# The last gather of every fourth block brought by SyncE's single-row copies instead of a GpSimd gather

## Chip, cores and metric

One core of one Trainium2 chip. The metric is the device time of one execution in microseconds (us). The kernel before takes 615.87 us, the median of 3 runs (612.99 to 616.21).

## What is computed

A recommendation model's top: for each of 2048 samples, 32 rows of 256 floats are taken from 32 embedding tables, all pairwise dot products of the 32 rows are formed, and three dense layers follow. Cut to what matters:

```python
e = jnp.stack([tbl_f[ids[:, f]] for f in range(32)], axis=1)     # [2048, 32, 256]
dots = jnp.einsum('bnd,bmd->bnm', e, e)
z = dots[:, iu, ju]                                               # pairs i < j: 496 numbers
h = jnp.concatenate([z, dense_ctx], axis=1)                       # with 16 dense inputs: 512
h = jnp.maximum(h @ W_top1 + b_top1, 0.0)
h = jnp.maximum(h @ W_top2 + b_top2, 0.0)
y = h @ W_top3
```

All in float32. The tables have 1000, 1250 or 12500 rows; 2048 random ids choose the rows.

## The kernel before, in words

The samples go through in 32 blocks of 64 (`BLOCK`). A block needs 64 x 32 rows of 1 KB. The fields go in units of four (`FPU`); a unit of a block is 256 rows and is fetched by two gathers (`SUBS`), each of 128 rows, one row to a partition. Blocks 0 to 3 have 8 units (`ALL`), so 16 gathers; from block 4 on there are 7 units (`UNITS`), 14 gathers, because the last four fields (`PICKS`, tables of 1000 rows) are fetched in another way: their tables lie on the chip, split into a high and a low part, and TensorE picks the rows by multiplying with one-hot matrices (`pick`). `unit(t, u)` numbers all units: there are 228, so 456 gathers.

POOL (GpSimd) issues the gathers, line 192, in order. Unit x goes into `rows[x % 8]`; from the ninth unit on POOL waits until PE has transposed unit x - 8 (line 190). The gather's row numbers are in `index`, which DVE makes once at the start by adding `base` to `raw` (`make_index`, line 403).

PE (TensorE) follows an order written out by hand (lines 292 to 316): for each unit it waits for its gathers and makes four transposes (line 205) into one of three PSUM buffers (`TURNS`), and between units it does a part of other work: the dot products of the block before (`gram`, line 252), the picks for blocks four ahead (lines 234, 236), and once in two blocks layers 1 to 3 (lines 268, 279, 286). Layer 1 of turn n comes in block 2n + 3 at unit 1; layer 3 of turn n in block 2n + 4 at unit 4. ACT (ScalarE) copies each transposed unit out of PSUM (line 327) and also, in one fixed order with it, spreads the ids that the picks need (`spread_ids`, line 339), takes the picks out of PSUM (line 343, `take_pick`) and puts them in place (line 350). In block 2n + 4, ACT spreads ids after unit 3 and takes a pick after unit 4; PE's pick at unit 6 waits for that copy. DVE makes the one-hots (line 410), regroups the dot products (line 422), and takes the scores (line 441).

SP (SyncE) issues all ordinary DMAs on one queue, in order. At the start: `base` and the first index part (lines 129, 131), the rest (line 132), tables 0 and 1 (line 140), ids 0 and 1 (line 136), two dense loads (line 144), table 2, the weights; then, after a wait for `low_done`, table 3. Then comes a loop of 16 turns, one for two blocks:

```python
for n in range(TILES):
    if n + 2 < JOBS // 2:
        sp.wait_ge(ids_spread, 2 * (n + 1))
        load_ids(n + 2)
    if n + 2 < TILES:
        sp.wait_ge(l1_done, n + 1)
        load_dense(n + 2)
    sp.wait_ge(score_ready, n + 1)
    sp.dma_start(out[n:n + 1, :], score[:, n % 2, :]).then_inc(stored[n % 2], 16)
```

`JOBS // 2` is 14, so turns 0 to 11 load ids. The ids loaded in turn n are first spread in block 2n + 4 after unit 3; turn n begins when score n - 1 is stored, which is in block 2n + 2.

Of the kernel before, what the change touches and what calls it, by code (L numbers as in the profile page):

```python
# [8 lines left out]
U32 = mybir.dt.uint32  # L9
ALU = mybir.AluOpType  # L10
ACT = mybir.ActivationFunctionType

P = 128
# [3 lines left out]
FPU = 4  # L17
# [2 lines left out]
GROUP = 256  # L20


def dlrm_tower(nc, index_t, base_t, pick_ids, pick_tables, dense_t, table, w1_t, b1_t, w2, b2_t, w3_t, out):

# [3 lines left out]
    D = table.shape[1]  # L30
# [4 lines left out]
    UNITS = (N_FIELDS - PICKS) // FPU  # L35
    SUBS = BLOCK // SPG
    GATHERS = ALL * SUBS
    BLOCKS = index_t.shape[1] // GATHERS
    FQ, TQ = BLOCK // QUAD, P // QUAD
    TILES = BLOCKS // 2  # L40
    BPG = GROUP // BLOCK
# [4 lines left out]
    VC = 8  # L46
    VP = V // VC
    ROWS, COLS, TURNS = 8, 3, 3
    PIECES = VC * D // 512
    assert HALVES == 2 and ND <= N_FIELDS and VP * VC == V and VP <= P and BPG == PICKS == 4  # L50

    def units(t):
        return ALL if t < BPG else UNITS

    def unit(t, u):
        return ALL * min(t, BPG) + UNITS * max(t - BPG, 0) + u

    def gram_parts(t):
        return {2: (0, 4), 3: (4, 8), 4: (8, 12), 5: (12, 16)} if t % 2 == 1 else {1: (0, 6), 2: (6, 11), 3: (11, 16)}

    with ExitStack() as ctx:
        def sb(name, shape, dt=F32):
            return ctx.enter_context(nc.sbuf_tensor(name, shape, dt))
# [4 lines left out]
        def sem(name):  # L68
            return ctx.enter_context(nc.semaphore(name))

        raw = sb("raw", [P, BLOCKS, GATHERS], U32)
        base = sb("base", [P, GATHERS], U32)
        index = sb("index", [P, BLOCKS, GATHERS], U32)
        rows = [sb(f"rows{r}", [P, SUBS, D]) for r in range(ROWS)]
        cols = [sb(f"cols{r}", [P, HALVES, BLOCK, N_FIELDS]) for r in range(COLS)]
        stage = [sb(f"stage{g}", [P, HALVES, GROUP, PICKS]) for g in range(2)]
        pairs = [sb(f"pairs{p}", [P, KC, P]) for p in range(2)]
# [8 lines left out]
        identity = sb("identity", [P, P])  # L86
# [16 lines left out]

        index_loaded = [sem(f"index_loaded{i}") for i in range(2)]
        index_ready = sem("index_ready")
        gathered = [sem(f"gathered{r}") for r in range(ROWS)]
        transposed, cols_ready = sem("transposed"), sem("cols_ready")
        gram_done, pairs_ready = sem("gram_done"), sem("pairs_ready")
# [18 lines left out]
        @block.sync  # L127
        def _(sp):
            sp.dma_start(base[:, :], base_t).then_inc(index_loaded[0], 16)
            index_v = index_t.rearrange("p (t g) -> p t g", t=BLOCKS)  # L130
            sp.dma_start(raw[:, 0:1, :], index_v[:, 0:1, :]).then_inc(index_loaded[0], 16)
            sp.dma_start(raw[:, 1:BLOCKS, :], index_v[:, 1:BLOCKS, :]).then_inc(index_loaded[1], 16)

            def load_ids(m):
                g, j = m // 2, 2 * (m % 2)
                sp.dma_start(pick_id[m % 2][:, :, :], pick_ids[g, j:j + 2, :].unsqueeze(0).broadcast_to([VP, 2, GROUP])
                             ).then_inc(ids_loaded[m % 2], 16)

            def load_table(j):
                sp.dma_start(table_raw[j], pick_tables[j].rearrange("(p c) d -> p c d", c=VC)  # L140
                             ).then_inc(table_loaded[j], 16)

            def load_dense(n):
                sp.dma_start(pairs[n % 2][0:ND, 0, :], dense_t[n]).then_inc(dense_loaded[n % 2], 16)

            load_table(0)
            load_table(1)
            load_ids(0)
            load_ids(1)
            sp.wait_ge(pairs_zeroed, 2)  # L150
            load_dense(0)
            load_dense(1)
            sp.wait_ge(table_loaded[0], 16)
            load_table(2)
            sp.wait_ge(table_loaded[1], 16)
            sp.dma_start(w1_sb[:, :, :], w1_t).then_inc(w1_loaded, 16)
            sp.dma_start(b1_sb[:, :], b1_t).then_inc(w_loaded, 16)
            sp.dma_start(b2_sb[:, :], b2_t).then_inc(w_loaded, 16)
            sp.dma_start(w3_sb[:, :], w3_t).then_inc(w_loaded, 16)
            sp.dma_start(w2_sb[:, :, :], w2.rearrange("(m p) n -> p m n", p=P)).then_inc(w_loaded, 16)  # L160
            sp.wait_ge(low_done, 3 * PIECES)
            load_table(3)
            for n in range(TILES):
                if n + 2 < JOBS // 2:
                    sp.wait_ge(ids_spread, 2 * (n + 1))
                    load_ids(n + 2)
# [5 lines that stand above are left out]
            for p in range(2):  # L172
                sp.wait_ge(stored[p], 16 * (TILES // 2))

        @block.gpsimd
        def _(pool):
            pool.memset(identity[:, :], 0.0).then_inc(identity_zeroed, 1)
            pool.iota(row_number[:, :], [[1, VC]], base=0, channel_multiplier=VC,
                      allow_small_or_imprecise_dtypes=True).then_inc(numbers_ready, 1)
            pool.wait_ge(identity_zeroed, 1)  # L180
            pool.affine_select(out=identity[:, :], in_=identity[:, :], compare_op=ALU.not_equal, fill=1.0,
                               base=0, pattern=[[-1, P]], channel_multiplier=1).then_inc(identity_ready, 1)
            pool.wait_ge(index_ready, 1)
            for t in range(BLOCKS):
                if t == 1:
                    pool.wait_ge(index_ready, 2)
                for u in range(units(t)):
                    x = unit(t, u)
                    if x >= ROWS:
                        pool.wait_ge(transposed, x - ROWS + 1)  # L190
                    for k in range(SUBS):
                        pool.indirect_dma_start(  # L192
                            out=rows[x % ROWS][:, k, :], out_offset=None, in_=table,
                            in_offset=bass.IndirectOffsetOnAxis(ap=index[:, t, SUBS * u + k:SUBS * u + k + 1], axis=0),
                        ).then_inc(gathered[x % ROWS], 16)

        @block.tensor
        def _(pe):
            def transposes(x):
                pe.wait_ge(gathered[x % ROWS], 16 * SUBS * (x // ROWS + 1))  # L200
                if x >= TURNS:
                    pe.wait_ge(cols_ready, x - TURNS + 1)
                for h in range(HALVES):
                    for k in range(SUBS):
                        last = pe.transpose(ps_turn[x % TURNS][:, h, SPG * k:SPG * (k + 1), :],  # L205
                                            rows[x % ROWS][:, k, h * P:(h + 1) * P], identity[:, :])
                last.then_inc(transposed, 1)

            def split_table(j):
# [5 lines left out]
                hi_v = table_hi[:, j, :, :].rearrange("p c d -> p (c d)")  # L215
                for i in range(PIECES):
                    x = PIECES * j + i
                    if x >= 2:
# [6 lines left out]
            def pick(q, h):  # L225
                j = q % PICKS
                if h == 0:
                    pe.wait_ge(one_hot_ready, q + 1)
                    if q < PICKS:
                        pe.wait_ge(lo_ready, PIECES * (3 if j < 2 else 4))  # L230
                    if q >= 1:
# [40 lines left out]
            def layer2(n):  # L272
                pe.wait_ge(hidden1_ready, n + 1)
                if n == 0:
                    pe.wait_ge(w_loaded, 64)
                    pe.wait_ge(lo_ready, PIECES * PICKS)
                for m in range(M2C):
# [122 lines left out]
        def _(dve):  # L400
            def make_index(t0, t1):
                n = t1 - t0
                dve.tensor_tensor(index[:, t0:t1, :], raw[:, t0:t1, :],
                                  base[:, :].unsqueeze(1).broadcast_to([P, n, GATHERS]), ALU.add).then_inc(index_ready, 1)
# [39 lines left out]
                dve.memset(pairs[p][0:N_FIELDS, 0, :], 0.0).then_inc(pairs_zeroed, 1)  # L444
            dve.wait_ge(index_loaded[0], 32)
            make_index(0, 1)
            dve.wait_ge(index_loaded[1], 16)
            make_index(1, BLOCKS)
            dve.wait_ge(numbers_ready, 1)

            def take_lo(j):
                for i in range(PIECES):
                    x = PIECES * j + i
                    dve.wait_ge(low_done, x + 1)
                    dve.tensor_copy(table_lo[:, j, :, :].rearrange("p c d -> p (c d)")[:, 512 * i:512 * (i + 1)],  # L455
                                    ps_low[x % 2]).then_inc(lo_ready, 1)
# [72 lines left out]
```

## Time and profile before

| | |
|---|---|
| median of 3 runs | 615.87 us |
| the profiled execution | 614.14 us, of which its span 612.3 us |
| PE, PEld busy | 522.7 us (85%), 466.6 us (76%) |
| POOL busy | 432.1 us (71%) |
| DVE, ACT busy | 278.3 us (45%), 209.6 us (34%) |
| DMA engines, mean busy share in the steady part | 3 to 4 tenths |
| granted TensorE clock, mean | 0.964 of full speed |

PE is TensorE's matmuls, PEld its weight loads, DVE VectorE, ACT ScalarE, POOL GpSimd, SPq SyncE's DMA queue. A matmul's end is modelled, so a busy PE is not PE at its peak. "Issue" is time in which an engine waited for nothing that the profile shows. The span is the time from the first to the last instruction of the profiled execution.

### The profile page before, as it was taken

To read this page: it belongs to the slowest core of one execution; us is meant where nothing else is said; L and a number is where in the kernel's file an instruction comes from. 1 tells how busy PE (TensorE), PEld (TensorE's weight loads), DVE (VectorE), ACT (ScalarE), POOL (GpSimd) and SP (SyncE) were. 2 spreads that over 40 slices of the span, in tenths; PEclk is the share of its full clock that TensorE was granted. 3 is DMA by queue.
4 is the path that set the end of the run, shared out by engine and by line. 5 is a ranking of instruction groups with operands and counts; after the bars stand their busy time and mean duration, and the time that the engine had idled before them with its cause. 6 is when DMAs were issued, how large, how long until landed. Compare 5 with 4: busy or idle time off the path is not lost.

```text
span 612.3 us, 24786 instructions
## 1 busy us (share of the span) xinstructions
PE 522.7 (85%) x11392; PEld 466.6 (76%) x11392; DVE 278.3 (45%) x600; ACT 209.6 (34%) x390; POOL 432.1 (71%) x463
## 2 busy tenths in 40 slices
PE   1068998999999999988999898989989897996967
PEld 0054796998889897978889786978878796984857
DVE  0013744827364545555273535556263555426060
ACT  1044233343433334343334224333332333432130
POOL 6767677777777777777777777777777777777600
PEclk9978998999999999998999999999999999998788
DMA  5695443443434343433434343434434333333300
GB/s 155 210 241 191 136 139 107 110 126 107 122 111 125 109 121 112 125 107 108 124 110 123 106 126 111 122 107 112 125 105 122 109 109 108 107 108 111 97 3 1
DMA packets 26411, 72.10 MB, mean 118 GB/s; under 512 B 8426, under 2 KB 9338, under 8 KB 25680
## 3 DMA queue, kind: packets, MB, share of 16 engines
q0 software_dynamic: 21888, 59.80, 35.5%
q1 hardware_dynamic: 4420, 10.72, 5.6%
q8 instruction: 90, 1.47, 1.0%
q14 instruction: 13, 0.11, 0.0%
HBM read 70.48 MB, written 0.01 MB: 115 GB/s over the span
## 4 chain that ended last, share of the span: by engine, by line
PE 65%; DMA 14%; POOL 11%; issue 7%; ACT 1%; DVE 1%; SPq 0%; POOLq 0%; ACTq 0%
PE ps_l L268 18%; PE ps_turn L205 15%; POOL rows L192 11%; PE ps_gram L252 11%; DMA rows<-in_table,index 10%; PE ps_pick L234 7%; PE ps_pick L236 7%; DMA pick_id<-in_pick_ids 5%; PE ps_l L279 2%; PE ps_l L220 1%; PE ps_pick L220 1%; PE ps_l L286 1%; DVE pairs L422 0%; PE ps_l L222 0%; PE ps_pick L222 0%
## 5 line engine op out<-in xcount | busy, mean ns | idle before, releaser
L192 POOL DMA_INDIRECT rows<-in_table,index x456 | 431.2, 946 | 146.3 <-issue 118.8
L422 DVE COPY pairs<-ps_gram 32x112 f32<-32x112 f32 (+1 forms) x504 | 189.1, 375 | 140.9 <-PE ps_gram L252 134.5
L327 ACT COPY cols<-ps_turn 128x512 f32<-128x512 f32 x228 | 132.1, 590 | 314.5 <-PE ps_turn L205 314.1
L205 PE MATMUL ps_turn<-identity,rows 128*128 128x128 f32 x912 | 148.2, 293 | 59.0 <-DMA rows<-in_table,index 44.6
L205 PEld LDWEIGHTS ps_turn<-identity,rows 128*128 128x128 f32 x912 | 104.0, 147 | 74.8 <-DMA rows<-in_table,index 41.2
L252 PE MATMUL ps_gram<-cols 128*32 128x32 f32 x8192 | 113.5, 201 | 22.9 <-issue 21.3
L252 PEld LDWEIGHTS ps_gram<-cols 128*32 128x32 f32 x8192 | 93.4, 111 | 49.9 <-issue 44.4
L410 DVE TENSOR_TENSOR one_hot<-ps_ids,row_number 125x2048 fp32r<-125x2048 f32 x28 | 63.9, 2281 | 139.5 <-ACT ps_ids L339 118.9
L268 PE MATMUL ps_l<-pairs,w_sb 128*128 128x128 f32 x1024 | 121.9, 282 | 3.1 <-DVE score L441 3.1
L268 PEld LDWEIGHTS ps_l<-pairs,w_sb 128*128 128x128 f32 x1024 | 120.5, 199 | 3.6 <-DVE pairs L422 3.6
L234 PE MATMUL ps_pick<-one_hot,table_hi 125*128 125x256 f32 x448 | 115.1, 295 | 0.4 <-ACT stage L343 0.4
L236 PE MATMUL ps_pick<-one_hot,table_lo 125*128 125x256 f32 x448 | 110.2, 284 | 0.0
L234 PEld LDWEIGHTS ps_pick<-one_hot,table_hi 125*128 125x128 f32 x448 | 86.1, 192 | 0.6 <-issue 0.6
L236 PEld LDWEIGHTS ps_pick<-one_hot,table_lo 125*128 125x128 f32 x448 | 86.5, 193 | 0.0
L343 ACT COPY stage<-ps_pick 128x512 f32<-128x512 f32 x28 | 30.6, 1093 | 37.0 <-PE ps_pick L236 37.0
L279 PE MATMUL ps_l<-hidden,w_sb 128*128 128x128 f32 x256 | 31.4, 276 | 1.2 <-ACT hidden L360 1.2
L279 PEld LDWEIGHTS ps_l<-hidden,w_sb 128*128 128x128 f32 x256 | 29.8, 192 | 1.6 <-ACT hidden L360 1.4
L360 ACT ACTIVATE hidden<-ps_l,b_sb 128x128 f32<-128x128 f32 x64 | 18.3, 376 | 10.4 <-PE ps_l L268 10.4
L339 ACT CAST ps_ids<-pick_id 125x256 f32<-125x256 int32 x28 | 10.7, 383 | 28.5 <-DMA pick_id<-in_pick_ids 28.5
L455 DVE CAST table_lo<-ps_l 125x512 fp32r<-125x512 f32 x8 | 5.5, 691 | 29.7 <-PE ps_l L222 29.7
L350 ACT COPY cols<-stage 128x512 f32<-128x512 f32 x28 | 17.4, 622 | 0.2
L433 DVE TENSOR_SCALAR hidden<-ps_l,b_sb 128x128 f32<-128x128 f32 x32 | 9.8, 347 | 13.9 <-PE ps_l L279 13.4
(31 smaller groups left out, 79.1 us busy)
## 6 DMA issues: line engine op xcount, KB each, us to landing
rows<-in_table,index POOLq DMA_INDIRECT x456
pick_id<-in_pick_ids SPq DMA_DIRECT2D x14, 250.0 KB
w_sb<-in_w_t SPq DMA_DIRECT2D x1, 2048.0 KB, 29.9
cols<-in_tbl SPq DMA_DIRECT2D x2, 1000.0 KB
stage<-in_tbl SPq DMA_DIRECT2D x2, 1000.0 KB
w_sb<-in_W_top SPq DMA_DIRECT2D x1, 512.0 KB, 32.6
pairs<-in_dense_t SPq DMA_DIRECT2D x16, 8.0 KB
scores<-score SPq DMA_DIRECT2D x16, 0.5 KB
```

What stands on the lines that cost most here:

```text
L192: pool.indirect_dma_start(out=rows[x % ROWS][:, k, :], out_offset=None, in_=table, in_offset=bass.IndirectOffsetOnAxis(ap=index[:, t, SUBS ...
L205: last = pe.transpose(ps_turn[x % TURNS][:, h, SPG * k:SPG * (k + 1), :], rows[x % ROWS][:, k, h * P:(h + 1) * P], identity[:, :])
L234: pe.matmul(ps_pick[:, h, :], table_hi[:, j, c, h * P:(h + 1) * P], one_hot[q % 2][:, c, :], start=(c == 0), stop=False)
L236: last = pe.matmul(ps_pick[:, h, :], table_lo[:, j, c, h * P:(h + 1) * P], one_hot[q % 2][:, c, :], start=False, stop=(c == VC - 1))
L252: last = pe.matmul(ps_gram[b % 2][N_FIELDS * j:N_FIELDS * (j + 1), g, :], x, x, start=(h == 0), stop=(h == HALVES - 1))
L268: last = pe.matmul(ps_l1[:, m, :], w1_sb[:, c, m * P:(m + 1) * P], pairs[n % 2][:, c, :], start=(c == 0), stop=(c == KC - 1))
L279: last = pe.matmul(ps_l1[:, m, :], w2_sb[:, c, m * P:(m + 1) * P], hidden1[:, c, :], start=(c == 0), stop=(c == M1C - 1))
L327: act.copy(cols[t % COLS][:, :, :, FPU * u:FPU * (u + 1)], ps_turn[x % TURNS][:, :, :, :]).then_inc(cols_ready, 1)
L343: act.copy(stage[q // PICKS % 2][:, :, :, q % PICKS], ps_pick[:, :, :]).then_inc(stage_ready, 1)
L360: last = act.activation(hidden1[:, m, :], ps_l1[:, m, :], ACT.Relu, bias=b1_sb[:, m:m + 1])
L410: dve.tensor_tensor(one_hot[q % 2][:, :, :], ps_ids[0:VP, :].unsqueeze(1).broadcast_to([VP, VC, GROUP]), row_number[:, :].unsqueeze(2).bro ...
L422: last = dve.tensor_copy(pairs[n % 2][N_FIELDS * q:N_FIELDS * (q + 1), c0:KC, TQ * j + FQ * u:TQ * j + FQ * (u + 1)] .rearrange("p c g -> ...
```

## The change

SP gets its own small list of row numbers: those of the last gather (unit 6, second half) of blocks 7, 11, 15, ... 31, seven lists of 128. DVE adds their base once. POOL leaves these seven gathers out. SP brings their rows in the first 14 turns of its loop, 64 rows in each turn (two turns to a block): it loads 8 row numbers into registers, issues 8 copies of one row each (1 KB from the table to one partition of `single_rows`), and so on 8 times. This stands ahead of the turn's ids load, dense load and store. There are two buffers `single_rows`, and from the third block on a wait for the transposes of the block whose buffer is written again. PE waits for these copies beside the gather, and reads `single_rows` for that half unit. To make room, `index` is now `raw` itself (added to in place).

```diff
-        index = sb("index", [P, BLOCKS, GATHERS], U32)
+        index = raw
+        single_raw = sb("single_raw", [1, SINGLES], U32)
+        single_base = sb("single_base", [1, FPU], U32)
+        single_index = single_raw
         rows = [sb(f"rows{r}", [P, SUBS, D]) for r in range(ROWS)]
+        single_rows = [sb(f"single_rows{e}", [P, D]) for e in range(2)]
...
+    def is_single(x, k):
+        return k == SUBS - 1 and any(x == unit(t, UNITS - 1) for t in range(2 * BPG - 1, BLOCKS, BPG))
+
+    def gathers_up_to(x):
+        return sum(not is_single(y, k) for y in range(x % ROWS, x + 1, ROWS) for k in range(SUBS))
...
+            sp.dma_start(single_raw[:, :], single_t).then_inc(index_loaded[1], 16)
+            sp.dma_start(single_base[:, :], single_base_t).then_inc(index_loaded[1], 16)
             load_table(0)
             load_table(1)
...
+            sp.wait_ge(index_ready, 3)
             for n in range(TILES):
+                e = n // 2
+                t = BPG * (e + 2) - 1
+                if t < BLOCKS:
+                    if n % 2 == 0 and e >= 2:
+                        sp.wait_ge(transposed, unit(t - 2 * BPG, UNITS - 1) + 1)
+                    for p0 in range(P // 2 * (n % 2), P // 2 * (n % 2 + 1), BATCH):
+                        _, numbers = nc.values_load_multi_w_load_instructions(
+                            single_index[0:1, P * e + p0:P * e + p0 + BATCH], engines=[mybir.EngineType.SP])
+                        for p, row in enumerate(numbers, p0):
+                            sp.dma_start(single_rows[e % 2][p:p + 1, :], table[bass.ds(row, 1), :]
+                                         ).then_inc(singles_loaded[e % 2], 16)
                 if n + 2 < JOBS // 2:
...
                     for k in range(SUBS):
+                        if is_single(x, k):
+                            continue
                         pool.indirect_dma_start(
...
-                pe.wait_ge(gathered[x % ROWS], 16 * SUBS * (x // ROWS + 1))
+                pe.wait_ge(gathered[x % ROWS], 16 * gathers_up_to(x))
+                e = (x - unit(2 * BPG - 1, UNITS - 1)) // (BPG * UNITS)
+                if is_single(x, SUBS - 1):
+                    pe.wait_ge(singles_loaded[e % 2], 16 * P * (e // 2 + 1))
...
+                        arrived = single_rows[e % 2][:, :] if is_single(x, k) else rows[x % ROWS][:, k, :]
...
-            dve.wait_ge(index_loaded[1], 16)
+            dve.wait_ge(index_loaded[1], 48)
             make_index(1, BLOCKS)
+            single_v = single_raw[:, :].rearrange("p (n f) -> p n f", f=FPU)
+            dve.tensor_tensor(single_v, single_v,
+                              single_base[:, :].unsqueeze(1).broadcast_to([1, SINGLES // FPU, FPU]), ALU.add
+                              ).then_inc(index_ready, 1)
```

`BATCH` is 8, `SINGLES` is 896. The host prepares `single_t` (the 896 ids) and `single_base_t` (the four tables' first rows).

## Rows read from the trace of the kernel before

**Rows 1.** The page, the chain that ended last, shares by line.
```profile
PE ps_l L268 18%; PE ps_turn L205 15%; POOL rows L192 11%; PE ps_gram L252 11%; DMA rows<-in_table,index 10%; PE ps_pick L234 7%; PE ps_pick L236 7%; DMA pick_id<-in_pick_ids 5%; PE ps_l L279 2%; PE ps_l L220 1%; PE ps_pick L220 1%; PE ps_l L286 1%; DVE pairs L422 0%; PE ps_l L222 0%; PE ps_pick L222 0%
```

**Rows 2.** The gathers' group on the page; POOL's waits (us, times, longest).
```profile
L192 POOL DMA_INDIRECT rows<-in_table,index x456 | 431.2, 946 | 146.3 <-issue 118.8
...
POOL rows L192 <- PE ps_turn L205: 25.5, 65, 2.6
```

**Rows 3.** Timeline of POOL: start us, us, instruction, idle before it and releaser.
```profile
3.46 1.10 POOL L192 DMA_INDIRECT rows<-in_table,index  x1 [2.05 <-DVE index L403]
...
33.22 0.94 POOL L192 DMA_INDIRECT rows<-in_table,index  x1 [2.40 <-PE ps_turn L205]
...
61.99 0.94 POOL L192 DMA_INDIRECT rows<-in_table,index  x1 [1.58 <-PE ps_turn L205]
...
66.80 0.94 POOL L192 DMA_INDIRECT rows<-in_table,index  x1 [2.62 <-PE ps_turn L205]
...
578.00 0.95 POOL L192 DMA_INDIRECT rows<-in_table,index  x1 [0.30 <-issue]
```

**Rows 4.** Stretches from score to score: length, PE, PEld, DVE, ACT, POOL busy (instructions), clock, DMA.
```profile
186.80:219.30 32.50, 31.43 (x718) 28.85 (x717) 17.39 (x38) 13.22 (x26) 24.58 (x27) 1.00 0.41 116
...
391.80:426.80 35.00, 31.27 (x719) 28.81 (x718) 17.37 (x39) 13.38 (x26) 26.47 (x29) 1.00 0.43 116
```

**Rows 5.** Timeline of PE at its last wait for rows.
```profile
568.25 1.12 PE L205 MATMUL ps_turn<-identity,rows 128*128 128x128 f32 x4 [1.29 <-DMA rows<-in_table,index]
```

**Rows 6.** PE's waits for gathered rows, from 233 to 569, then from 550 to 569.
```profile
PE ps_turn L205 <- DMA rows<-in_table,index: 23.6, 26, 1.9
...
PE ps_turn L205 <- DMA rows<-in_table,index: 7.3, 8, 1.5
```

**Rows 7.** Timeline of SP's queue at the start.
```profile
1.22 0.42 SPq L131 DMA_DIRECT2D raw<-in_index_t  x1
1.69 0.42 SPq L132 DMA_DIRECT2D raw<-in_index_t  x1
```

**Rows 8.** The chain that ended last, in order of time: its longest early piece.
```profile
2.90 27.90 DMA pick_id<-in_pick_ids
```

**Rows 9.** Timeline of DVE at the start.
```profile
4.32 0.68 DVE L403 CUSTOM_DVE_ANT_0 index<-base,raw 128x992 uint16<-128x992 uint16 x1 [1.15 <-DMA raw<-in_index_t]
```

**Rows 10.** DMA packets, MB and share from 610.5 to 612.3, with one store.
```profile
q1 hardware_dynamic: 2, 0.00, 0.1%
...
scores<-score SPq DMA_DIRECT2D x1, 0.5 KB
```

**Rows 11.** Timeline of SP's queue in the loop.
```profile
120.65 0.24 SPq L171 DMA_DIRECT2D scores<-score  x1
...
356.03 0.24 SPq L171 DMA_DIRECT2D scores<-score  x1
356.31 0.26 SPq L136 DMA_DIRECT2D pick_id<-in_pick_ids  x1
...
426.81 0.24 SPq L171 DMA_DIRECT2D scores<-score  x1
...
461.32 0.26 SPq L136 DMA_DIRECT2D pick_id<-in_pick_ids  x1
...
532.28 0.24 SPq L171 DMA_DIRECT2D scores<-score  x1
```

**Rows 12.** DMA issues by line: queue, form, count, KB, us to landing.
```profile
base<-in_base_t SPq DMA_DIRECT2D x1, 8.0 KB, 1.7
```

**Rows 13.** Timeline of ACT in block 20.
```profile
382.78 0.38 ACT L339 CAST ps_ids<-pick_id 125x256 f32<-125x256 int32 x1
385.84 0.58 ACT L327 COPY cols<-ps_turn 128x512 f32<-128x512 f32 x1 [2.68 <-PE ps_turn L205]
387.75 1.09 ACT L343 COPY stage<-ps_pick 128x512 f32<-128x512 f32 x1 [1.32 <-PE ps_pick L236]
```

**Rows 14.** SP's packets, MB and share from 465 to 466 us.
```profile
q1 hardware_dynamic: 19, 0.03, 11.1%
```

**Rows 15.** Timeline of PE in block 20, the pick at unit 6.
```profile
389.02 0.37 PE L234 MATMUL ps_pick<-one_hot,table_hi 125*128 125x256 f32 x1
```

**Rows 16.** The page, the queue of the gathers: packets, MB, share of 16 engines.
```profile
q0 software_dynamic: 21888, 59.80, 35.5%
```

More of the change, by code:

```diff
@@ L20, with dlrm_tower @@
 GROUP = 256
-def dlrm_tower(nc, index_t, base_t, pick_ids, pick_tables, dense_t, table, w1_t, b1_t, w2, b2_t, w3_t, out):
+def dlrm_tower(nc, index_t, base_t, single_t, single_base_t, pick_ids, pick_tables, dense_t, table, w1_t, b1_t, w2, b2_t, w3_t, out):
     D = table.shape[1]
@@ L48, in dlrm_tower @@
     ROWS, COLS, TURNS = 8, 3, 3
+    SINGLES, BATCH = single_t.shape[1], 8
     PIECES = VC * D // 512
@@ L105, in dlrm_tower @@
         index_ready = sem("index_ready")
+        singles_loaded = [sem(f"singles_loaded{e}") for e in range(2)]
         gathered = [sem(f"gathered{r}") for r in range(ROWS)]
@@ L204, in transposes @@
                     for k in range(SUBS):
+                        arrived = single_rows[e % 2][:, :] if is_single(x, k) else rows[x % ROWS][:, k, :]
                         last = pe.transpose(ps_turn[x % TURNS][:, h, SPG * k:SPG * (k + 1), :],
-                                            rows[x % ROWS][:, k, h * P:(h + 1) * P], identity[:, :])
+                                            arrived[:, h * P:(h + 1) * P], identity[:, :])
                 last.then_inc(transposed, 1)
@@ L502 @@
     index_t = ids[:, order].reshape(blocks, BLOCK // SPG, SPG, units, FPU).transpose(2, 4, 0, 3, 1)
+    single = index_t.reshape(P, blocks, -1)[:, 7::4, 13].T.reshape(1, -1)
+    single_t = dram("single_t", single.astype(np.uint32))
+    single_base_t = dram("single_base_t", starts[24:28].reshape(1, FPU))
     index_t = dram("index_t", index_t.reshape(P, -1).astype(np.uint32))
@@ L524 @@
     out = nc.dram_tensor("scores", (tiles, P), F32, kind="ExternalOutput").ap()
-    dlrm_tower(nc, index_t, base_t, pick_ids, pick_tables, dense_t, table, w1_t, b1_t, w2, b2_t, w3_t, out)
+    dlrm_tower(nc, index_t, base_t, single_t, single_base_t, pick_ids, pick_tables, dense_t, table, w1_t, b1_t, w2, b2_t, w3_t, out)
     result = run_bass_kernel_spmd(nc, [arrays], core_ids=[0])
```

## Prediction

> **What bounds the kernel now.** I read the page's chain first: it runs mostly through PE, but 21% of the span is POOL and the DMA of the rows [rows 1]. So PE works while something at POOL decides when a part of it may start. The second view is who POOL waits for. It has 456 gathers of 0.946 us, and of its 146.3 us of idle time 118.8 is "issue", about 0.30 ahead of each gather; it is put down to PE 65 times, 25.5 us in all, mostly the same 0.30 [rows 2]. The timeline confirms this: starts lie 1.25 us apart from 3.46 to the last at 578.00, and only three are late, by 2.1, 1.3 and 2.3 us over the 0.30 [rows 3]. 455 steps of 1.25 and 5.7 are 574.5, which is 578.00 - 3.46. **POOL is never held up after 66.8 us; its 1.25 us per gather sets the pace.** Two blocks are 28 gathers, 35.0 us, and late scores lie that far apart. PE alone needs less: while it still works off rows gathered ahead, two blocks take it 32.5 us, with as many matmuls (718 against 719 in the 35.0) [rows 4]. It last starves at 568.25, ahead of unit 1 of block 31 [rows 5]; a layer-1 job of 64 matmuls follows, behind which the last rows land. From there the tail is PE's.
>
> **What is removed.** Seven gathers, in blocks 7, 11, ... 31. That of block 31 comes after 568.25, where rows no longer hold PE: worth nothing. Six precede it: 6 x 1.25 = 7.5 us. PE can follow, for from 233 us, where the starving begins in earnest, to 569 it waits 23.6 us for rows [rows 6]; of these it then waits 7.5 less. The 7.5 counts in full.
>
> **What is added at the start.** Two loads on SP ahead of the first tables, 0.42 us each and 0.05 between [rows 7]: 0.9 us. The chain's longest early piece is the landing of the first ids, to 30.8 [rows 8], and POOL's late start at 33.22 hangs on it: I charge 0.9 (ends 0 and 0.9). The added one-partition sum on DVE is like the 992-wide one, 0.68 us [rows 9]; DVE then has nothing until the first ids, so it is hidden, and uncovered it would cost its 0.7. The index written in place is the same instruction with another target; POOL needs it 20 us later, at block 1.
>
> **What SP now does.** In the first 14 turns of its loop, ahead of the ids load, it makes 8 register loads and issues 64 copies; call their time X. A copy is shaped like the score store: one partition, 2 packets, so one DMA engine [rows 10]. That issues in 0.24 us, and the next DMA starts 0.28 after it [rows 11]. Two prices are in no row. *Address arithmetic on registers*: below 0 (done within the copy), above 0.30 a copy (POOL's issue gap, the widest that repeats); I take 0.08, two steps of SP's own gap of 0.04, the same engine's. *A register load of 8 numbers*: below 0.04, above 1.7 us, a small DMA from issue to landing [rows 12]; I take 0.42, SP's dear issue [rows 7], since it waits for an answer but crosses no DMA queue. X = 64 x (0.28 + 0.08) + 8 x 0.42 = 26.4 us; ends 18.2 and 50.7.
> The Trainium skill (DMA: Bandwidth & Descriptors, section Latency and other measured facts) puts the floor of a register load at about 600 ns; by that X would be 27.8 and the sum 614.7, no gain. No trace here shows such a load.
>
> **Who waits behind SP.** Queued behind the copies are the ids load, the dense load and the store. Ids: issued at 356.31 [rows 11], used by ACT at 382.78 [rows 13]. They land after 4.2 us: those issued at 461.32 have their last packets between 465 and 466 [rows 11, 14]. So X may be 382.78 - 356.31 - 4.2 = 22.3 before ACT is late. ACT has 4.0 more: 0.38 + 0.58 of work ahead of the copy of PE's pick at 387.75, which takes 1.09 and releases PE's next pick at 389.02 [rows 13, 15]. Free up to 26.3.
> Beyond, it recurs. From a score to that pick: 0.28 + X + 4.2 + 0.38 + 0.58 + 1.09 + 0.18 = X + 6.7. From that pick to the next score: 426.81 - 389.02 = 37.8 [rows 11, 15], less the 2.5 that PE starves in such a pair of blocks, 35.3. Two turns thus take at least X + 42, and the score at 532.28, twelve turns behind that at 120.65 [rows 11], comes no earlier than 120.65 + 6(X + 42) = 372.7 + 6X. POOL allows it at 532.28 - 7.5 + 0.9 = 525.7, and PE's later waits for rows, 7.3 us after 550 [rows 6], let it catch up. So lateness reaches the end beyond X = (525.7 + 7.3 - 372.7)/6 = 26.7, and **each us of X over that costs 6 us**. My 26.4 is just inside. A dense load is used two turns on, a score buffer free again two turns on: both hidden, with the same 26 us of cover. The copied rows are due at the end of every fourth block: turn 13 starts its copies near 525 and ends by 553, before POOL's own last rows near 571; here even X = 40 is hidden.
>
> **DMA.** A copy's 2 packets go to one engine, which is 41 to 43% busy otherwise [rows 4]. Ends for the two: 0.03 us (the store's, 0.1% of 16 engines for 1.8 us, [rows 10]) and 0.32 (twice the gathers' mean packet, 35.5% x 16 x 612.3 / 21888 = 0.159, [rows 16]). At 0.1 to 0.2 it is hidden behind 0.41 of issue. The bytes are those of the gather removed.
>
> **Sum.** 614.14 (the profiled execution, 1.8 outside its span) - 7.5 + 0.9 = 607.5. The median before is 1.7 above that execution, so 609.2 in the runs: **609**, 1.1% faster.
>
> **Rivals.**
> 1. *The ids come late* (slower). Three steps of arithmetic and loads of 0.7 us give X = 64 x 0.40 + 8 x 0.7 = 31.2: 607.5 + 6 x 4.5 = 634.5, in the runs 636. It decides from X = 28.3, 0.44 us a copy with all in it. For it: the sum leaves 0.3 us of room, and both open prices can be higher. Against: the stores issue evenly at 0.24. Chance 0.25.
> 2. *A copy with a register address issues like SP's first loads*, 0.47 instead of 0.28 [rows 7]: X = 64 x 0.55 + 3.4 = 38.6, so 607.5 + 71.4 = 678.9, in the runs 681. Against it: the store of the same shape takes half. Chance 0.10. The Trainium skill (DMA: Bandwidth & Descriptors, section Why a DMA increments its semaphore by 16 and not by 1, the table's column for earlier generations) has 512 sequencer cycles for a DMA instruction, and Advanced Engine Details and Errata (Clock Domains) a 1.2 GHz sequencer: 0.43 us. The 0.24 of rows 11 speaks against it for a fixed address; none shows a register's.
> 3. *No change.* X from 27.2 to 28.2 gives back 3 to 9 us: 610.5 to 616.5. Or gathers land later behind copies on the one engine: at 0.32 us each in the 58% left, 0.55 a copy, X is 35 and this joins rival 1; at half of that a part of the 7.5 goes. Chance 0.15.
> 4. That POOL isn't lightened is excluded: seven instructions of a serial engine are gone.
>
> **How the numbers follow.** Forecast 0.50, rival 1 0.25, rival 2 0.10, rival 3 0.15. About 0.5% (3.1 us) is what a measurement of this kernel tells from no change. Faster 0.50, same 0.15, slower 0.35. Low end: nothing charged at the start and the runs' median as far below as before's lowest (2.9), 604. High end: X = 33 gives 607.5 + 37.8 + 1.7 = 647, rounded to 648, which leaves out rival 2 and the upper part of 1, under 0.2. The forecast's own range is 604 to 612.
>
> **What would show it.** Right: POOL has 449 gathers 1.25 us apart, its last near 571; SP's 64 copies take at most 26 us; ACT's use of the ids waits for no DMA; PE still waits for rows in the last 50 us. Wrong: copies over 0.44 us apart with the loads shared out, ACT or PE waiting behind the ids' DMA, POOL waiting for PE's transposes, scores 36 us or more apart.

## The result: 8% slower, and the profile after

The changed kernel takes 665.91 us (median of 4 runs, 661.16 to 668.69), the kernel before beside it 616.04 us. The ratio is 1.082, interval 1.078 to 1.086. The forecast was 609, the range 604 to 648. The profiled execution took 667.21 us with a span of 665.4 us.

In the new kernel's numbering line 220 is the gather, 185 the register load, 188 the single-row copy, 148 the ids load, 197 the score store, 237 the transposes, 266 and 268 the picks, 371 the spreading of the ids and 375 ACT's copy of a pick. First the page: the granted clock in 40 slices, the chain by engine and by line, and the gathers' group.

```profile
PEclk9979999987999969998899979999698996999998
...
PE 46%; SPq 23%; issue 12%; DMA 10%; DVE 7%; ACT 2%; POOL 0%; ACTq 0%
SPq L188 17%; PE ps_l L300 11%; PE ps_gram L284 10%; PE ps_turn L237 9%; DMA pick_id<-in_pick_ids 8%; DVE pairs L454 6%; SPq L185 6%; PE ps_pick L266 5%; PE ps_pick L268 5%; PE ps_l L311 3%; DMA rows<-in_table,raw 2%; PE ps_l L252 1%; PE ps_pick L252 1%; ACT stage L375 1%; ACT cols L359 1%
...
L220 POOL DMA_INDIRECT rows<-in_table,raw x449 | 424.6, 946 | 206.2 <-issue 119.2
```

POOL has lost its seven gathers and has gone from the chain, where POOL and the rows' DMA held 21% [rows 1]; the rows are left with 2%. SP's queue holds 23% in their place, with the copies (17%) and their register loads (6%). The clock line has single slices at 6, which steady slices of before did not have. The waits say the same (who waited, for whom: us in all, times, longest):

```profile
ACT ps_ids L371 <- DMA pick_id<-in_pick_ids: 132.2, 12, 30.0
POOL rows L220 <- PE ps_turn L237: 84.9, 57, 7.0
PE ps_pick L266 <- ACT stage L375: 57.9, 8, 10.9
```

POOL now really waits for PE, up to 7.0 us at a time, against 2.6 before [rows 2]. ACT waits for ids 12 times (the longest, 30.0 us, is the first load's, at the start), and PE for ACT's copy of a pick. SP's timeline over one pair of turns shows who starts it:

```profile
278.28 0.24 SPq L197 DMA_DIRECT2D scores<-score  x1
279.51 32.80 SPq L188 DMA_DIRECT2D single_rows<-in_table  x64
312.37 0.27 SPq L148 DMA_DIRECT2D pick_id<-in_pick_ids  x1
...
313.06 0.27 SPq L197 DMA_DIRECT2D scores<-score  x1
314.33 32.37 SPq L188 DMA_DIRECT2D single_rows<-in_table  x64
346.75 0.27 SPq L148 DMA_DIRECT2D pick_id<-in_pick_ids  x1
...
355.78 0.24 SPq L197 DMA_DIRECT2D scores<-score  x1
```

Before, the ids load stood 0.28 us behind the store [rows 11]; now it is 34.1 us behind (312.37 - 278.28), so X was 33.8 us where I had 26.4. ACT and PE at the end of that wait:

```profile
316.67 0.38 ACT L371 CAST ps_ids<-pick_id 125x256 f32<-125x256 int32 x1 [13.76 <-DMA pick_id<-in_pick_ids]
316.98 0.58 ACT L359 COPY cols<-ps_turn 128x512 f32<-128x512 f32 x1
317.46 1.08 ACT L375 COPY stage<-ps_pick 128x512 f32<-128x512 f32 x1
```

```profile
318.68 0.55 PE L266 MATMUL ps_pick<-one_hot,table_hi 125*128 125x256 f32 x1 [9.24 <-ACT stage L375]
```

It is the loop that I had written down: store, X, landing, ids, evacuation, copy of the pick, and then PE, which has stood 9.24 us. From store to late pick it takes 40.8, 39.7, 40.4, 41.2, 40.1 and 40.3 us in the six pairs of turns, 40.4 in the mean; my formula X + 6.7 gives 40.5. Only one of two turns stalls PE so: in the other the score is ready before SP is.

Where X went wrong is seen inside SP. The chain has one copy after another in pieces, and the instructions' own durations (ns, min/median/max) are:

```profile
280.39 0.23 SPq L188
280.62 0.05 issue
280.67 0.04 SPq L188
280.71 0.04 issue
280.74 0.03 SPq L188
280.77 0.03 issue
280.80 0.23 SPq L188
```

```profile
L188 SPq FUSED_REGOPS  x896: 37/37/46, 68.8 to 627.3; - x180
L188 SPq MOVE single_rows<-in_table x896: 29/29/38, 68.8 to 627.4; - x180
L188 SPq DMA_DIRECT2D single_rows<-in_table x896: 224/225/314, 68.9 to 627.4; - x180
...
L185 SPq TENSOR_LOAD <-single_raw x112: 688/783/950, 67.9 to 623.6; - x112
```

A copy is a fused register operation, a move and the DMA, 0.41 us from one to the next. A register load of 8 numbers takes 0.78. Eight copies and their load mostly come round every 4.10 us, which leaves 0.82 for the load. I had 0.36 and 0.42. Eight such rounds are 32.8 us; the last 1.0 us of X is longer rounds. The turn shown above has a load of 0.95 us and two pauses of 0.3 us between copies, of which this is one (the gap is otherwise 0.05):

```profile
289.77 0.34 issue
```

What causes the pauses is not shown.

### The profile page after: what moved, and what is told of

It is laid out like the page before. It is cut to its first block, busy times and chain, and to the rows that moved or that the text cites. A ratio compares the mean times of both kernels' runs of the same rounds, so it can differ in the third digit from the quotient of the medians.

```text
span 665.4 us, 27584 instructions
## 1 busy us (share of the span) xinstructions
PE 532.2 (80%) x11392; PEld 478.9 (72%) x11392; DVE 279.0 (42%) x601; ACT 207.7 (31%) x390; POOL 425.5 (64%) x456
## 4 chain that ended last, share of the span: by engine, by line
PE 46%; SPq 23%; issue 12%; DMA 10%; DVE 7%; ACT 2%; POOL 0%; ACTq 0%
SPq L188 17%; PE ps_l L300 11%; PE ps_gram L284 10%; PE ps_turn L237 9%; DMA pick_id<-in_pick_ids 8%; DVE pairs L454 6%; SPq L185 6%; PE ps_pick L266 5%; PE ps_pick L268 5%; PE ps_l L311 3%; DMA rows<-in_table,raw 2%; PE ps_l L252 1%; PE ps_pick L252 1%; ACT stage L375 1%; ACT cols L359 1%
## 5 line engine op out<-in xcount | busy, mean ns | idle before, releaser
L220 POOL DMA_INDIRECT rows<-in_table,raw x449 | 424.6, 946 | 206.2 <-issue 119.2
L237 PE MATMUL ps_turn<-identity,rows 128*128 128x128 f32 x898 | 145.1, 292 | 38.0 <-DMA rows<-in_table,raw 23.2
L266 PE MATMUL ps_pick<-one_hot,table_hi 125*128 125x256 f32 x448 | 125.4, 313 | 57.9 <-ACT stage L375 57.9
L284 PE MATMUL ps_gram<-cols 128*32 128x32 f32 x8192 | 118.7, 200 | 27.5 <-issue 24.5
L266 PEld LDWEIGHTS ps_pick<-one_hot,table_hi 125*128 125x128 f32 x448 | 94.1, 210 | 59.6 <-issue 59.6
L284 PEld LDWEIGHTS ps_gram<-cols 128*32 128x32 f32 x8192 | 96.5, 110 | 56.1 <-issue 50.1
L300 PE MATMUL ps_l<-pairs,w_sb 128*128 128x128 f32 x1024 | 119.0, 278 | 5.1 <-DVE score L473 5.1
L300 PEld LDWEIGHTS ps_l<-pairs,w_sb 128*128 128x128 f32 x1024 | 117.5, 194 | 5.6 <-DVE pairs L454 5.6
L268 PE MATMUL ps_pick<-one_hot,table_lo 125*128 125x256 f32 x448 | 119.9, 301 | 0.0
L268 PEld LDWEIGHTS ps_pick<-one_hot,table_lo 125*128 125x128 f32 x448 | 94.4, 211 | 0.0
```

Source lines behind the costliest of these rows:

```text
L220: pool.indirect_dma_start(out=rows[x % ROWS][:, k, :], out_offset=None, in_=table, in_offset=bass.IndirectOffsetOnAxis(ap=index[:, t, SUBS ...
L266: pe.matmul(ps_pick[:, h, :], table_hi[:, j, c, h * P:(h + 1) * P], one_hot[q % 2][:, c, :], start=(c == 0), stop=False)
L268: last = pe.matmul(ps_pick[:, h, :], table_lo[:, j, c, h * P:(h + 1) * P], one_hot[q % 2][:, c, :], start=False, stop=(c == VC - 1))
L284: last = pe.matmul(ps_gram[b % 2][N_FIELDS * j:N_FIELDS * (j + 1), g, :], x, x, start=(h == 0), stop=(h == HALVES - 1))
L300: last = pe.matmul(ps_l1[:, m, :], w1_sb[:, c, m * P:(m + 1) * P], pairs[n % 2][:, c, :], start=(c == 0), stop=(c == KC - 1))
```

## The experiments

Times are medians, ratios are to the kernel before in the same rounds. I held three theories, which the expectations call by their letters. **A**: the loss is the ids load that waits behind the copies. **B**: the copies disturb by themselves (their packets, the gathers' landing). **C**: SP's turn is too long as a whole.

**The ids load first**, the copies behind it:

```diff
             for n in range(TILES):
+                if n + 2 < JOBS // 2:
+                    sp.wait_ge(ids_spread, 2 * (n + 1))
+                    load_ids(n + 2)
                 e = n // 2
...
-                if n + 2 < JOBS // 2:
-                    sp.wait_ge(ids_spread, 2 * (n + 1))
-                    load_ids(n + 2)
```

> The changed kernel with one thing moved: in each turn of SP's loop the ids load stands ahead of the 64 copies. Theory A (the loss is the ids load that waits behind 33.8 us of copies): the wait of ACT for the ids and PE's stalls at the pick go; SP's turn of about 34.5 us fits POOL's 34.4 for two blocks, so 607 to 612 us. Theory B (the copies themselves disturb, by their packets on one DMA engine or by delaying gathers): nothing moves, 660 to 668. Theory C (SP's whole turn of copies, dense load and store is too long and its other work, not the ids, holds the others): 630 to 668.

607.94 us, ratio 0.9905 (0.9878 to 0.9931): the whole loss is gone and the forecast gain is there, with every copy still made. So the loss is not the copies' own disturbance, and B falls. SP's timeline, and PE's wait for ACT at the pick:

```profile
367.88 0.27 SPq L197 DMA_DIRECT2D scores<-score  x1
368.19 0.26 SPq L148 DMA_DIRECT2D pick_id<-in_pick_ids  x1
369.46 32.50 SPq L191 DMA_DIRECT2D single_rows<-in_table  x64
402.01 0.33 SPq L156 DMA_DIRECT2D pairs<-in_dense_t  x1
402.39 0.27 SPq L197 DMA_DIRECT2D scores<-score  x1
...
PE ps_pick L266 <- ACT stage L375: 0.4, 1, 0.4
```

SP's turn is 34.5 us here, and in these turns SP's store of the score follows its dense load at once, so C is close to binding without doing so.

**The gathers left out, nothing brought** (the copies, PE's wait for them and the use of `single_rows` removed from the changed kernel; it leaves out 896 rows, and PE transposes what lies in their place):

> POOL's seven gathers left out and no copies in their place (those 896 rows are never brought; PE transposes what the half unit's buffer holds). It measures POOL's part alone. Theory A: 6 gathers of 1.25 us count, less 0.9 at the start: 607 to 608. Rival (PE or the tail takes the gain back): 611 to 616.

607.6 us, ratio 0.9901 (0.9865 to 0.9937). POOL's part, with the charge at the start, is worth what the sum gave it, 607.5. The run with the ids first, 607.94 us with all copies made, can't be told from it, so there the copies cost nothing measurable, by the gathers' landing or otherwise.

**All gathers kept beside the copies** (`is_single` no longer skips them on POOL, `gathers_up_to` counts all), run twice, the second time beside the changed kernel:

> The changed kernel with POOL's seven gathers kept as well, so the rows come twice and POOL isn't lightened. Theory A (the ids set the pace, POOL has room): as the changed kernel, 664 to 669. Rival (POOL is still on the path beside it): 7 us more than the changed kernel, 673 to 676.

670.69 us, ratio 1.0901 (1.0856 to 1.0946), between the two expectations. So:

> The changed kernel itself, beside the next one and on the same chip, so that the two can be compared: 663 to 669.

> All gathers kept on POOL beside the copies, again. The first time it took 670.7, between theory A (664 to 669) and its rival (673 to 676). If POOL has no part in the changed kernel's end, it is within 2 us of the run before this one; if its seven gathers still cost, 5 to 8 us above it.

668.83 us (1.0834 to 1.0943) and 670.41 us (1.0865 to 1.0959). They differ by 1.6 us with intervals that lie over one another (the first measurements, from different rounds, by 4.8): in the changed kernel POOL's 7.5 us are worth at most a part of that, and what they are worth can't be told from nothing.

**Fewer copies**, 48 and 56 of each 64 rows, to vary X alone. The other rows are left out: their partitions are set to zero once at the start, and PE waits for fewer copies.

```diff
-                    for p0 in range(P // 2 * (n % 2), P // 2 * (n % 2 + 1), BATCH):
+                    for p0 in range(P // 2 * (n % 2), P // 2 * (n % 2) + 48, BATCH):
```

> Only 48 of the 64 rows of each turn are copied (the other 16 partitions of each half stay zero, two small memsets on DVE at the start), so SP's block before the ids load is 6 x 4.1 + 1.0 = 25.6 us instead of 33.8. Theory A with its threshold at 26.7 us: no loss, 607 to 611. Theory B (loss in proportion to the copies): 0.75 of the loss of 58 us remains, about 651.

> As the run with 48, now 56 of 64 rows a turn: SP's block before the ids load is 7 x 4.1 + 1.0 = 29.7 us, 3.0 over the threshold of 26.7. Theory A: 607.5 + 6 x 3.0 = 625, with up to 1.8 us more for each of six stalls if TensorE's clock falls in them, so 623 to 638. Theory B: 0.875 of the loss of 58 us, about 658; but the 48 copies already cost almost nothing. A jump to 660 or more would say that the loss isn't in proportion to the wait.

609.57 us (ratio 0.9925, 0.9895 to 0.9956) and 641.44 us (1.0471, 1.0428 to 1.0513). PE's waits at the pick, first with 48, then with 56:

```profile
PE ps_pick L266 <- ACT stage L375: 13.5, 10, 3.1
```

```profile
PE ps_pick L266 <- ACT stage L375: 37.5, 7, 7.5
```

From store to ids it is 25.5 and 29.7 us, so X is 25.2 and 29.4. Three quarters of the copies cost some 2 us (against no copies), the next eighth 32, the last eighth 24 or more: between these two values of X lies a threshold, and the computed 26.7 is inside. The runs don't place it closer. 641.44 is 3 us over the range that I had given this run.

**Sixteen numbers to a register load** (`BATCH` 16):

> The changed kernel with 16 row numbers to a register load instead of 8, so 4 loads a turn instead of 8. If a load of 16 takes as long as one of 8 (0.78 us and 0.05 beside it), SP's block falls from 33.8 to 30.5 us: theory A gives 607.5 + 6 x 3.8 = 630, with the clock up to 641. If a load's time goes with its numbers, nothing changes: 664 to 668.

658.24 us, ratio 1.0694 (1.066 to 1.0729). That is between the two expectations. The load of 16 takes longer, so 32.1 to 32.5 us are left from store to ids, not 30.8; and again the time is above the formula, which gives 638.

```profile
L185 SPq TENSOR_LOAD <-single_raw x56: 1218/1230/1319, 68.8 to 609.8; - x56
```

**Copies without registers**, in the kernel before (with `index` in place too). In each of 14 turns SP makes 120 single-row copies from fixed addresses into a buffer `spare` that nobody reads, first ahead of the ids load, then behind it:

```diff
+                if n < 14:
+                    if n >= 2:
+                        sp.wait_ge(spare_loaded[n % 2], 16 * 120 * (n // 2))
+                    for p in range(120):
+                        sp.dma_start(spare[n % 2][p:p + 1, :], table[P * n + p:P * n + p + 1, :]
+                                     ).then_inc(spare_loaded[n % 2], 16)
```

> The kernel before with all gathers on POOL, plus, ahead of the ids load in each of 14 turns, 120 single-row copies from fixed addresses (no registers) into a spare buffer that nobody reads: 120 x 0.28 = 33.6 us of SP, as long as the 64 copies with register loads. Theory A (only the time that SP is occupied ahead of the ids load counts): the same loss, 662 to 672. Rival D (register loads or register addresses disturb in some other way): near 615.

> As the run with 120 copies from fixed addresses ahead of the ids load, but behind it: SP is as busy, the engine 0 of the DMA gets as many packets, only the ids load doesn't wait. SP's turn is then 36.3 + 0.9 = 37.2 us, longer than POOL's 35.0 for two blocks, so from the turns on SP itself sets the ids' pace: 14 turns from 66.4 end at 587 instead of the scores' 564. Theory A with that cap: the last ids load (turn 11) is issued near 475 to 480 against 461, not late by more than its room; 614 to 622. Theory B (the copies disturb): near 680.

682.44 us (1.1129, 1.1094 to 1.1163) ahead, 620.25 us (1.0098, 1.0071 to 1.0126) behind. Neither registers nor a changed POOL are needed for the loss; an SP that is occupied ahead of the ids load is enough. 682 is above the 662 to 672 expected: a copy took 0.30 us and not 0.28, which is 2.4 us in X and by the formula 14 in all, as the timeline of the first of the two shows:

```profile
281.14 0.24 SPq L179 DMA_DIRECT2D scores<-score  x1
281.43 35.99 SPq L170 DMA_DIRECT2D spare<-in_table  x120
317.46 0.26 SPq L138 DMA_DIRECT2D pick_id<-in_pick_ids  x1
```

Store to ids is 36.3 us. The 1% that the run behind loses agrees with theory C. SP's turn is 37.2 us there against POOL's 35, so SP falls back a little in each turn, and near the end PE waits once for the last dense load, which stands behind 120 copies, longer than the 6 us that the run loses. No other run has this wait:

```profile
PE ps_l L277 <- DMA pairs<-in_dense_t: 8.6, 1, 8.6
```

**The rest, about 18 us.** With the measured X my formula gives 607.5 + 6 x (33.8 - 26.7) = 650.1, and the profiled execution took 667.2. In its trace the excess is in one place, the stretch from late pick to next score. It takes 38.2, 38.6, 37.1, 38.5, 40.2 and 37.8 us, 38.4 in the mean, where I had 35.3. Six times 3.1 is 18.6. (In the trace of the changed kernel's second measurement, 669.42 us, the same stretch takes 37.3 us in the mean, which is 12 us in all, and the first score came 4.1 us later, so the split varies from execution to execution.) The first lines show the 3.5 us behind two of the six late picks (columns as in rows 4; the other four have 16 matmuls and 0.50 too), the last the same pick of the kernel before:

```profile
318.68:322.18 3.50, 3.50 (x16) 3.50 (x17) 0.69 (x1) 1.28 (x3) 0.00 (x0) 0.50 0.13 36
...
556.04:559.54 3.50, 3.50 (x16) 3.50 (x17) 0.69 (x1) 1.28 (x3) 0.00 (x0) 0.50 0.02 7
```

```profile
389.02:392.52 3.50, 3.50 (x32) 3.50 (x31) 3.39 (x9) 1.50 (x3) 2.67 (x3) 1.00 0.36 97
```

After a stall of 8 to 11 us TensorE works on at a granted 0.50 (1.2 GHz) and does 16 matmuls where it did 32. Over the whole stretches from late pick to next score the granted clock was 0.91 to 0.95, as in the third and the fifth:

```profile
318.68:355.78 37.10, 35.88 (x740) 33.43 (x741) 15.92 (x38) 13.47 (x27) 20.86 (x23) 0.95 0.32 89
475.56:515.75 40.19, 37.65 (x742) 35.20 (x743) 15.95 (x38) 13.91 (x27) 23.28 (x25) 0.91 0.33 90
```

A mean of 0.95 is a tenth of the time at 0.50, half of which is lost where TensorE is the limit: 1.9 us of 37.1. My estimate from the six mean clocks is 14 us lost in all, of the 18.6. In the fifth stretch, the longest, the clock fell a second time, to 0.51 from 503.4 to 506.8. To test the clock's part, matmuls that serve nothing were put into the stalls:

```diff
+                    if t % 4 == 2 and 6 <= t <= 26 and u == 6:
+                        pe.wait_ge(pairs_ready, t - 1)
+                        for _ in range(64):
+                            pe.matmul(ps_gram[t % 2][:, 0:4, :].rearrange("p g f -> p (g f)"), w1_sb[:, 0, 0:P], w1_sb[:, 1, 0:P], start=True, stop=True)
```

> The changed kernel with 64 matmuls of 128 columns that serve nothing (they write a free PSUM buffer that is overwritten later), put ahead of the pick of unit 6 in blocks 6, 10, 14, 18, 22 and 26, where PE stalls 8 to 11 us for the late ids and the granted clock falls to 0.50, where it stays for some 3 to 4 us of work after the stall. Theory A2 (the changed kernel is 16 to 20 us over my formula partly because of this clock): the granted clock stays higher behind the stall, each pair of turns is about 2 us shorter, 652 to 658. Rival (the clock has no part in it): 664 to 668, or more by some us if 7 us of matmuls don't fit the stall.

678.95 us, ratio 1.1049 (1.0995 to 1.1103), slower than the changed kernel and far outside what I expected if the clock counts. The 64 matmuls left 128 records and took some 14.3 us, longer than the stall. As a test it still speaks: with the clock at 1.00 throughout, pick to score took 36.0, 36.6, 35.1, 36.6, 35.9 and 35.1 us, mean 35.9, against 38.4. The window of the third, which begins 0.26 us behind the start of the pick:

```profile
327.10:362.00 34.90, 34.15 (x741) 31.66 (x741) 15.28 (x37) 12.46 (x24) 20.80 (x22) 1.00 0.32 91
```

Then with 34 of them:

> As the run with 64 idle matmuls in each stall, with 34 instead: 34 x 0.223 = 7.6 us, inside the stalls of 7.7 to 10.9 us. If the low clock is the excess, picks start when they did and each of six pairs of turns is 2 to 3.5 us shorter: 648 to 657. If it isn't, 664 to 669.

655.04 us, ratio 1.0684 (1.0651 to 1.0716), against ratios of 1.082 and 1.0889 for the changed kernel: 8 to 13 us less, clear of the intervals. More work on PE, less time. In its trace the picks come as late as before, but PE stands idle 1.7 to 4.2 us instead of 8 to 11, and pick to score takes 36.9 us in the mean. Behind the four longer rests (3.1 to 4.2 us) the clock is still down, behind the two short ones (1.7 and 2.7) it is not; one of each:

```profile
322.84:326.34 3.50, 3.50 (x18) 3.50 (x19) 0.69 (x1) 1.28 (x3) 0.00 (x0) 0.57 0.07 25
555.93:559.43 3.50, 3.50 (x30) 3.50 (x31) 0.69 (x1) 1.86 (x4) 0.64 (x1) 1.00 0.03 7
```

The length of the rest alone doesn't decide it. In this trace and in the changed kernel's the clock fell once more, to 0.51, from 496.6 to 500.0 and from 503.4 to 506.8 us, each time about the end of a rest of TensorE ahead of dot products (1.65 and 1.69 us). Why a rest of 1.7 us was followed by the lower clock there and not behind the pick is open.

**A version that beats both.** The ids first, and the two small start loads (with DVE's sum) moved behind the first ids loads, with 8 or 16 numbers to a register load:

```diff
-            sp.dma_start(single_raw[:, :], single_t).then_inc(index_loaded[1], 16)
-            sp.dma_start(single_base[:, :], single_base_t).then_inc(index_loaded[1], 16)
             load_table(0)
             load_table(1)
             load_ids(0)
             load_ids(1)
+            sp.dma_start(single_raw[:, :], single_t).then_inc(single_arrived, 16)
+            sp.dma_start(single_base[:, :], single_base_t).then_inc(single_arrived, 16)
```

> The run with the ids load first (8 numbers to a register load), with only the two small start loads moved behind the first ids loads. If they cost 0.9 us at the start, this is 0.9 us under the run with the ids first (ratio to before about 0.989); if not, the same 0.9905.

> The run with the ids load first, with 16 numbers to a register load and with the two small start loads moved behind the first ids loads. The 0.9 us charged at the start should go, and SP's turn be 31 us instead of 34.5: 606 to 608, at least 0.5 us under the run with the ids first, if that charge was real.

605.48 us (0.9877, 0.9847 to 0.9908) with 8, 606.3 us (0.9866, 0.9842 to 0.9889) with 16; the two can't be told apart. The intervals of the first and of the run with the ids first alone lie over one another, so the times don't prove the start charge; POOL's first late start does show it, 1.2 us earlier than in the run with the ids first and where it was before [rows 3]. The run with the ids first, then the late start loads:

```profile
34.32 0.94 POOL L220 DMA_INDIRECT rows<-in_table,raw  x1 [3.17 <-PE ps_turn L237]
```

```profile
33.14 0.94 POOL L221 DMA_INDIRECT rows<-in_table,raw  x1 [2.19 <-PE ps_turn L238]
```

## Why the prediction was wrong

**What held.** POOL's 1.25 us set the pace, and leaving out its gathers is worth what I gave it: measured alone, 0.9901 against 607.5 / 614.14 = 0.989. (The run can't tell six gathers from seven, 1.25 us apart.) The start charge was of the right size (1.2 for 0.9 us). The work behind the copies, and the loop store, X, landing, ACT, pick, were the right ones; store to pick was right within 0.1 us in the mean once X is put in. So was the slope of 6: in the turns ahead of the late picks store to ids is 29.7 us in the mean with 56 copies and 33.9 in the changed kernel, and the time went from 641.4 to 665.9 and, measured again, 668.8, which is 5.8 to 6.5 us for each. That the copies' own DMA work is hidden held too (the ids-first run).

**The step that failed** is the price of X, 26.4 us, which measured 33.8: its two unseen terms were too small, and that put X below the threshold of 26.7 instead of 7.1 above. The register load was put at 0.42 us "since it waits for an answer but crosses no DMA queue", and is 0.82 with its gaps: 8 x 0.40 = 3.2 us of the 7.4 missing. The arithmetic was put at "two steps of SP's own gap of 0.04". There are two steps, but each has a duration and a gap, 0.13 in all: 64 x 0.05 = 3.2. The rest, 1.0, is the longer rounds and pauses shown above. I noted that the sum left 0.3 us of room before 6 us are lost for each; with such a slope the likeliest time deserved no half of the chance, because both terms had been chosen near the low end of their bounds. (The sum with a register load of 600 ns comes to 614.3 by the same formula, not 614.7; nothing hangs on it.)

**Why even the range missed.** It ended at X = 33, near the true 33.8, and by the formula that is 647 and 652 in the runs. What lay above was a term that I didn't have: TensorE's clock behind each stall. In rows of before PE's waits for rows were at most 1.9 us in the steady part [rows 6], and the price of a stall was taken as its length. The stretch behind the late pick, put at 35.3 us, measured 38.4: 650.1 + 18.6 = 668.7, against 667.2 in the profiled execution. The clock's share of the 18.6 is some 14 to 15 us, by the mean clocks and by the 35.9 us that the stretch took at full clock; the other 3 to 4 us are not explained, and 35.3 was itself a little short.

**The rivals.** Rival 1 is what happened, with X = 33.8 for its 31.2 and the clock on top. Rival 2's time (681) was nearer than the forecast by luck, for its reason is wrong: the DMA instruction with a register address takes 0.225 us, no more than the store's 0.24 [rows 11]. That also decides the rule set beside it: the Trainium skill (DMA: Bandwidth & Descriptors, section Why a DMA increments its semaphore by 16 and not by 1) has 512 cycles for the DMA instruction, an estimate of 0.43 us as worked out in the prediction, and the measurement, about half of it, decides. The same page of the Trainium skill puts the floor of a register load at about 600 ns (Latency and other measured facts), and the trace's 0.69 to 0.95 for 8 numbers agrees. It would have been a better price than my row, and it spoke against the gain. Rival 3 took no part: X was far beyond its 28.2, and with the ids first the copies cost nothing measurable.

## What to carry to other kernels

When work is put on a queue that looks idle, the question is not whether the queue has room for it in a period but what stands behind it: put the short load that another engine waits for first and the long batch behind it; here that one move is the difference between 8% slower and 1% faster. Work out the point from which lateness goes round a loop and comes back each time, and if the estimate lies within the error of its unseen prices, forecast both sides alike. And price a stall of TensorE in the steady part as its length plus what the lower clock costs behind it, here some 2.4 us for each stall by my estimate.

## What the runs showed that I had not expected

A register load costs 0.78 us for 8 numbers and 1.23 for 16, so between the two it goes up by 0.056 for each number, and 16 to a load save under 2 us of 34. Address arithmetic for one dynamic copy is 0.13 us, a third of the copy. Behind stalls of 8 to 11 us the granted clock was 0.50 in all six; behind picks after rests of 1.7 and 2.7 us it stayed at 1.00. Thirty-four matmuls for nothing in each of six stalls made the kernel 8 to 13 us shorter. What stays open is why store to score varied between pairs (77.5 to 80.3 us): from the ids' issue to ACT's use of them it took 4.0 to 5.2 us, the longest pair had the second fall of the clock, and neither was tried by itself.
